# Graph attention with a layer norm in front: the normalisation moved from ScalarE to VectorE, and a batch of row statistics finished after the first weights

## The chip, the cores and the metric

The kernel runs on one core of one Trainium2 chip. The metric is the device time of one execution in microseconds (us). A core has TensorE (PE, matrix products and transposes), VectorE (DVE), ScalarE (ACT), GpSimd (POOL) and SyncE (SP); each works through its own list of instructions in order, and semaphores hold an instruction back until another engine has counted far enough. SyncE and GpSimd also start the transfers (DMA) between the chip's main memory and its on-chip memory (SBUF). PSUM is the memory that TensorE writes.

## The reference, cut to what matters

x is 8192 x 128, adj an 8192 x 8192 matrix of 0 and 1 (int32, about one entry in 512 is 1), W is 128 x 128 and a has 256 values.

```
h  = maximum(layernorm(x), 0)          # per row of 128, eps 1e-5
Wh = h @ W
f1, f2 = Wh @ a[:128], Wh @ a[128:]
e  = leaky_relu(f1[:, None] + f2[None, :], 0.2)
e  = where(adj == 0, -inf, e)
out = x + softmax(e, axis=1) @ Wh
```

## The kernel before, in words

**Tiling.** The 8192 rows are 64 tiles of 128, taken in 16 row groups of 4 tiles. The same 16 groups appear twice: as destination rows q (the rows of the output), and as source blocks b (the columns of adj that are summed over). For each pair (q, b), a "unit", TensorE transposes the adjacency marks of the block into PSUM (`transposes`, L266), VectorE turns them into weights with four instructions of 128 x 512 (`weights`, L601), and TensorE multiplies the weights with the features of the block and adds to four accumulators (`products`: 16 wide products of 258 columns at L277 and 16 of 129 columns at L281). There are 16 x 16 = 256 units.

**The first row of units, q = 0, also makes the features.** For a row group g the steps are, with the letters that the text uses:
- statistics (g): four `bn_stats` on VectorE, L548, on the loaded x.
- moments (k) and inverses (k): a batch k of groups is finished together. The batches are group 0; groups 1 to 3; 4 to 7; 8 to 11; 12 to 15. `moments` is five small VectorE instructions (L556 to L562), then ScalarE takes a logarithm and an exponential (`root`, L450 and L452), then `inverses` is four small VectorE instructions, each but the last waiting for the one in front (L570 to L575).
- normalise (g): four ScalarE activations of 128 x 128 float32 with a scale and a bias per partition, L395, from xm into one of two buffers xn. Buffer g mod 2 is free once group g-2 has been transposed.
- x_transposes (g): four PE transposes, L228. relu (g): one ScalarE instruction, L404.
- features (g, 0) and (g, 1): PE, L241, each followed by keep (g, h) on ScalarE, L410.
- exponentials (g): two ScalarE instructions, L422 and L423. pack (g): two small VectorE instructions, L583 and L584. spread (g): four PE transposes, L256. keep_row (g): ScalarE, L443.
- scaled (g): four ScalarE activations, L430. high_part (g): ScalarE, L437. low_part (g): VectorE, L592.

**What sets the order.** Each engine's order is written out by hand: a prologue, then `for b in range(UN)` with 16 turns, L319 for PE, L479 for ScalarE, L637 for VectorE. In turn b, here called block b, PE runs: transposes of block b+1, x_transposes (b+3), a wait for the weights and the pair of block b, then four parts of products with features (b+2, 0), spread (b+1) and features (b+2, 1) between them. spread (b+1) waits for pack (b+1) and for relu (b+3), because both write the same PSUM bank. ScalarE runs scaled (b+1), relu (b+3), high_part (b+1), keep (b+2, 0), keep_row (b+1), normalise (b+4), keep (b+2, 1), exponentials (b+2), and root at b = 3 and b = 7. VectorE runs statistics (b+8), weights (b+1), low_part (b+1), moments if b is 3 or 7, pack (b+2), inverses if b is 3 or 7. The batch of groups 4 to 7 has its statistics, moments and inverses in VectorE's prologue; ScalarE's root (2) for it stands in front of normalise (3) and of block 0's scaled (1) and relu (3).

**The loads.** SyncE loads x in five transfers, one for each batch; the fourth (groups 8 to 11) and the fifth are issued after the first four adjacency loads have landed (L158). GpSimd issues the adjacency loads, L181, 1 MB of int32 each, converted to 256 KB of bytes.

**The other rows of units,** q = 1 to 15, have no feature work: PE runs transposes of a block three ahead and the 32 products of a unit, VectorE the four weights, ScalarE copies the accumulators out (`evacuate`, L505).

Of the kernel before, what the change touches and what calls it, by code (L numbers as in the profile page):

```python
# [28 lines left out]
ALU = mybir.AluOpType  # L29
ACT = mybir.ActivationFunctionType  # L30
# [7 lines left out]
P = 128  # L38
PACK = 4
# [15 lines left out]
def gat_kernel(nc, x, adj, W, a, out):  # L55
# [3 lines left out]
    NQ = NB // PACK  # L59
# [10 lines left out]
    def batch_of(g):  # L70
        return next(k for k, (lo, hi) in enumerate(BATCHES) if lo <= g < hi)

    with ExitStack() as ctx:
# [10 lines left out]
        xm = sb("xm", [P, NQ, BANK], F32)  # L84
# [5 lines left out]
        xn = sb("xn", [P, 2, BANK], F32)  # L90
# [294 lines left out]
        @block.scalar  # L385
        def _(act):

            def normalise(g):

                act.wait_ge(s["ln_ready"], batch_of(g) + 1)  # L390
                if g >= 2:
                    act.wait_ge(s["xt_ready"], g - 1)
                for r in range(PACK):
                    t = g * PACK + r
                    mm = nc.scalar.activation(xn[:, g % 2, r * P:(r + 1) * P], xm[:, g, r * P:(r + 1) * P],  # L395
                                              ACT.Identity, scale=small[:, 5, t:t + 1], bias=small[:, 6, t:t + 1])
                mm.then_inc(s["xn_ready"], 1)

            def relu(g):

                act.wait_ge(s["xt_ready"], g + 1)
# [54 lines left out]
            act.wait_ge(s["wtp_ready"], 1)  # L456
            nc.scalar.activation(wt[:], acc[:, 0, 0:P], ACT.Copy).then_inc(s["wt_ready"], 1)
            root(0)
            normalise(0)
            nc.scalar.activation(squares, acc[:, 0, 0:P], ACT.Square,  # L460
                                 accum_out=lim[:, 2:3]).then_inc(s["norms_ready"], 1)
            relu(0)
            root(1)
            normalise(1)
            keep(0, 0)
            relu(1)
            keep(0, 1)
# [2 lines left out]
            high_part(0)  # L470
            keep_row(0)
            keep(1, 0)
            normalise(2)
            relu(2)
            keep(1, 1)
            exponentials(1)
            root(2)
            normalise(3)
            for b in range(UN):  # L479
                if b + 1 < NQ:  # L480
                    scaled(b + 1)
                if b + 3 < NQ:
                    relu(b + 3)
                if b + 1 < NQ:
                    high_part(b + 1)
                if b + 2 < NQ:
                    keep(b + 2, 0)
                if b + 1 < NQ:
                    keep_row(b + 1)
                if b + 4 < NQ:  # L490
                    normalise(b + 4)
                if b + 2 < NQ:
                    keep(b + 2, 1)
                    exponentials(b + 2)
                if b == 3 or b == 7:
                    root(3 + b // 7)
# [37 lines left out]
        def _(dve):  # L534
# [30 lines left out]
            def inverses(k):  # L565

                sl = slice(BATCHES[k][0] * PACK, BATCHES[k][1] * PACK)
                gap, both, total, root, square, rstd, shift = (small[:, n, sl] for n in range(7))
                dve.wait_ge(s["root_ready"], k + 1)
                then(nc.vector.tensor_tensor(square, root, root, ALU.mult))  # L570
                then(nc.vector.scalar_tensor_tensor(out=square, in0=square, scalar=-0.5, in1=both,
                                                    op0=ALU.mult, op1=ALU.mult))
                then(nc.vector.scalar_tensor_tensor(out=rstd, in0=square, scalar=1.5, in1=root,
                                                    op0=ALU.add, op1=ALU.mult))
                nc.vector.scalar_tensor_tensor(out=shift, in0=total, scalar=-0.5, in1=rstd,  # L575
                                               op0=ALU.mult, op1=ALU.mult).then_inc(s["ln_ready"], 1)


            def pack(g):

                dve.wait_ge(s["exps_ready"], g + 1)
                sl = slice(g * PACK, (g + 1) * PACK)
                then(nc.vector.tensor_scalar(packedv[:, sl, :, 1], exps[:, sl, :], CAP, CUT, ALU.min, ALU.mult))  # L583
                nc.vector.scalar_tensor_tensor(out=packedv[:, sl, :, 0], in0=exps[:, sl, :], scalar=CAP,  # L584
                                               in1=packedv[:, sl, :, 1], op0=ALU.min, op1=ALU.subtract
                                               ).then_inc(s["packed_ready"], 1)
# [30 lines left out]
            statistics(0)  # L617
            moments(0)
            inverses(0)
            dve.wait_ge(s["wap_ready"], 1)  # L620
            nc.vector.tensor_copy(wx[:, Fo:E1], acc[:, 1, 0:1]).then_inc(s["wx_ready"], 1)
            nc.vector.tensor_scalar(wx[:, E1:WC], acc[:, 1, 1:2], -1.0, None, ALU.mult).then_inc(s["wx_ready"], 1)
# [1 line left out]
                statistics(g)  # L624
            moments(1)
            inverses(1)
            pack(0)
            statistics(4)
            statistics(5)
            low_part(0)  # L630
            first_weights(0)
            pack(1)
            statistics(6)
            statistics(7)
            moments(2)
            inverses(2)
            for b in range(UN):  # L637
                if b + 8 < NQ:
                    statistics(b + 8)
                if b + 1 < NQ:  # L640
                    first_weights(b + 1)
                    low_part(b + 1)
                if b == 3 or b == 7:
                    moments(3 + b // 7)
                if b + 2 < NQ:
                    pack(b + 2)
                if b == 3 or b == 7:
                    inverses(3 + b // 7)
# [124 lines left out]
```

## Time and profile before

| what | value |
|---|---|
| time, median of 3 runs | 881.77 us (881.33 to 881.92) |
| the profiled execution's own time | 881.87 us |
| its span | 880.1 us |
| PE busy | 844.1 us, 96% of the span |
| VectorE busy | 756.4 us, 86% |
| ScalarE busy | 116.8 us, 13% |
| adjacency loads | 256 of 256 KB, 67.13 MB, 80.4% of 16 DMA engines' span |

The span is the time from the first to the last instruction of the profiled execution; its own time adds 1.77 us of what lies around. Busy shares are averages over the whole span. The stage in which the features are made fills the first 120.8 us, and in it ScalarE is busy most of the time; in the 742 us after it, ScalarE is nearly idle. "Idle before, released by" behind a row of a timeline means that the engine stood still for so long and what ended the wait. Rows that have "x4" are four instructions in a row: start of the first, then the length from there to the end of the last. An instruction's listed duration is about 0.08 us longer than the distance to the next one on VectorE, since they overlap at their ends.

### The profile page before, as it was taken

The page shows a single profiled execution, that of the slowest core. Times are in us where ns is not written, and L with a number is a line of the kernel's source. Part 1 is how long each engine was busy: PE and PEld are TensorE (multiplying, and loading weights), DVE is VectorE, ACT ScalarE, POOL GpSimd, SP SyncE. Part 2 cuts the span into 40 slices and gives each one's busy share as a digit, 9 for nine tenths or more (in the row PEclk, how much of TensorE's full clock was granted, in tenths as well). Part 3 has the DMA queues.
Part 4 walks back from the last instruction along what each step waited for, and adds up shares of the span by engine and source line. Part 5 has one row for each costly group of instructions (what it writes and reads, how often), then busy time and mean ns, then how long its engine had stood idle before and what let it go on. Part 6 is the DMA issues. An engine that isn't in the chain of part 4 may idle for free.

```text
span 880.1 us, 22961 instructions
## 1 busy us (share of the span) xinstructions
PE 844.1 (96%) x9475; PEld 773.2 (88%) x9475; DVE 756.4 (86%) x1287; ACT 116.8 (13%) x318; POOL 136.6 (16%) x263
## 2 busy tenths in 40 slices
PE   3699999999999999999999999999999999999995
PEld 2588899999999999999999999999999999999995
DVE  3588689898989889898989989898989989898985
ACT  4599930000000000000000000000000000000000
POOL 4000021111111111111111111111101110111000
PEclk9999999999999999999999999999999999999998
DMA  8995569899888988898899889988898989988400
GB/s 152 159 122 51 49 64 114 83 101 86 91 83 87 99 81 92 84 100 83 90 85 92 92 81 94 93 90 83 91 93 82 90 83 102 85 90 83 41 13 16
DMA packets 41740, 75.96 MB, mean 86 GB/s; under 512 B 4720, under 2 KB 4848, under 8 KB 41712
## 3 DMA queue, kind: packets, MB, share of 16 engines
q0 software_dynamic: 36864, 67.13, 80.4%
q1 hardware_dynamic: 4848, 8.46, 2.8%
q8 instruction: 18, 0.29, 0.1%
q14 instruction: 10, 0.08, 0.0%
HBM read 272.70 MB, written 4.19 MB: 315 GB/s over the span
## 4 chain that ended last, share of the span: by engine, by line
PE 88%; ACT 7%; issue 2%; DVE 2%; POOL 0%; DVEq 0%; POOLq 0%; ACTq 0%
PE acc L277 49%; PE acc L281 25%; PE stage L266 12%; ACT xn L395 3%; ACT tmp L430 1%; DVE wt_ring L601 1%; ACT wh L410 1%; ACT ht L404 1%; ACT pairs L437 1%; PE stage L241 1%; PE stage L228 1%; ACT exps L422 0%; PE stage L256 0%; ACT tmp L423 0%; DVE stats L548 0%
## 5 line engine op out<-in xcount | busy, mean ns | idle before, releaser
L601 DVE SCALAR_TENSOR_TENSOR wt_ring<-row,packed,stage 128x512 f32<-128x512 uint8 (+1 forms) x1024 | 695.4, 743 | 79.3 <-PE acc L281 68.2
L277 PE MATMUL acc<-pairs,wt_ring 128*128 128x258 f16 x4096 | 720.4, 274 | 0.4 <-DVE wt_ring L601 0.2
L281 PE MATMUL acc<-pairs,wt_ring 128*128 128x129 f16 x4096 | 698.5, 219 | 0.0
L277 PEld LDWEIGHTS acc<-pairs,wt_ring 128*128 128x128 f16 x4096 | 396.3, 97 | 55.6 <-DVE wt_ring L601 0.4
L281 PEld LDWEIGHTS acc<-pairs,wt_ring 128*128 128x128 f16 x4096 | 399.6, 98 | 4.9
L181 POOL DMA_DIRECT2D masks<-in_adj_dram x256 | 135.7, 536 | 658.2 <-PE stage L266 646.4
L266 PE MATMUL stage<-ident,masks 128*128 128x128 f32 x1024 | 155.0, 275 | 0.0
L505 ACT ACTIVATE fin<-acc 128x258 f32<-128x258 f32 x64 | 24.8, 387 | 730.2 <-PE acc L277 730.2
L266 PEld LDWEIGHTS stage<-ident,masks 128*128 128x128 f32 x1024 | 108.8, 141 | 3.7
L395 ACT ACTIVATE xn<-xm,small 128x128 f32<-128x128 f32 x64 | 26.2, 483 | 1.7 <-DVE small L575 1.7
L228 PE MATMUL stage<-ident,xn 128*128 128x128 f32 x64 | 12.3, 322 | 12.6 <-ACT xn L395 12.6
L241 PE MATMUL stage<-wx,ht 128*128 128x130 f32 x128 | 23.5, 311 | 0.7 <-ACT ht L404 0.7
L228 PEld LDWEIGHTS stage<-ident,xn 128*128 128x128 f32 x64 | 7.9, 159 | 15.6 <-ACT xn L395 15.6
L430 ACT ACTIVATE tmp<-wh,tmp 128x128 f32<-128x128 f32 x64 | 20.4, 390 | 0.4
L241 PEld LDWEIGHTS stage<-wx,ht 128*128 128x128 f32 x128 | 19.0, 213 | 1.6 <-ACT ht L404 1.1
L548 DVE BATCH_NORM_STATS2 stats<-xm 128x6 f32<-128x128 f32 x64 | 13.5, 279 | 7.3 <-DMA xm<-in_x_dram 7.3
L583 DVE TENSOR_SCALAR packed<-exps 128x8 f16<-128x8 f32 x16 | 2.8, 174 | 19.2 <-ACT tmp L423 19.2
L664 DVE SCALAR_TENSOR_TENSOR xm<-fin,inv,xm 128x128 f32 (+1 forms) x64 | 18.2, 348 | 0.0
L256 PE MATMUL stage<-ident,packed 128*128 128x128 f32 x64 | 10.8, 296 | 4.0 <-ACT ht L404 2.4
L654 DVE SCALAR_TENSOR_TENSOR fin<-fin 128x516 f32<-128x516 f32 x16 | 11.1, 691 | 3.4 <-ACT fin L505 3.4
L256 PEld LDWEIGHTS stage<-ident,packed 128*128 128x128 f32 x64 | 7.2, 147 | 6.8 <-issue 4.9
L410 ACT ACTIVATE wh<-stage 128x260 f32<-128x260 f32 x32 | 11.9, 371 | 2.9 <-PE stage L241 2.8
(44 smaller groups left out, 71.5 us busy)
## 6 DMA issues: line engine op xcount, KB each, us to landing
masks<-in_adj_dram POOLq DMA_DIRECT2D x256, 256.0 KB, 8.8
out_dram<-xm SPq DMA_DIRECT2D x16, 256.0 KB, 2.0
xm<-in_x_dram SPq DMA_DIRECT2D x3, 1024.0 KB, 17.5
xm<-in_x_dram SPq DMA_DIRECT2D x1, 768.0 KB, 6.4
xm<-in_x_dram SPq DMA_DIRECT2D x1, 256.0 KB, 2.6
wx<-in_L_gnn_W_dram SPq DMA_DIRECT2D x1, 64.0 KB, 2.4
a_sb<-in_L_gnn_a_dram SPq DMA_DIRECT2D x1, 1.0 KB, 3.8
```

Of the source, the lines that this page charges most:

```text
L181: nc.gpsimd.dma_start(masks[:, c * PACK + r, :], adj_dram[q, r, c]).then_inc(adj_loaded[c], 16)
L228: mm = nc.tensor.transpose(stage[:, 2, r * P:(r + 1) * P], xn[:, g % 2, r * P:(r + 1) * P], ident[:])
L241: mm = nc.tensor.matmul(stage[:, 3, r * 256:r * 256 + WC], ht[:, g % 2, k:k + P], wx[:], start=(r == 0), stop=(r == 1), skip_group_check=True)
L266: mm = nc.tensor.transpose(stage[:, bank, r * P:(r + 1) * P], words[:, c * PACK + r, kk * P:(kk + 1) * P], ident[:])
L277: return nc.tensor.matmul(acc[:, r, 0:2 * E1], wtv[:, w, r, 1, :], pairv[:, t, :, 0:E1], start=st, stop=end)
L281: return nc.tensor.matmul(acc[:, r, 0:E1], wtv[:, w, r, 0, :], pairv[:, t, 0, 0:E1], start=False, stop=False)
L395: mm = nc.scalar.activation(xn[:, g % 2, r * P:(r + 1) * P], xm[:, g, r * P:(r + 1) * P], ACT.Identity, scale=small[:, 5, t:t + 1], bias=s ...
L410: nc.scalar.activation(wh[:, t:t + 2, :], stage[:, 3, :].rearrange("p (r c) -> p r c", r=2)[:, :, 0:WC], ACT.Copy).then_inc(s["wh_ready"], 1)
L430: mm = nc.scalar.activation(tmp[:, g % 2, r, 0:Fo], wh[:, g * PACK + r, 0:Fo], ACT.Identity, scale=tmp[:, g % 2, r, Fo:E1])
L505: nc.scalar.activation(fin[:, r, :], acc[:, r, 0:2 * E1], ACT.Copy).then_inc(s["acc_free"], 1)
L601: nc.vector.scalar_tensor_tensor(out=wt_ring[:, t % NW, :], in0=e_row, scalar=packed[:, t, 1:2], in1=marks[:, k, :], op0=ALU.max, op1=ALU. ...
L664: nc.vector.scalar_tensor_tensor(out=o, in0=fin[:, r, 0:Fo], scalar=inv[:, r:r + 1], in1=o, op0=ALU.mult, op1=ALU.add).then_inc(s["rows_do ...
```

## The change

ScalarE's normalise is taken out at all its places and written as four VectorE `tensor_scalar` instructions, with the same waits and the same semaphore. In VectorE's prologue its order becomes: group 0 behind inverses (0), groups 1 and 2 behind inverses (1), group 3 behind the first weights; statistics (4) and (5) and low_part (0) are reordered around the first weights; inverses (2) leaves the prologue and goes behind weights (1) and low_part (1) in block 0. In the loop, statistics (b+8), which stood in front of the weights, goes behind them and behind normalise (b+4).

```diff
@@ ScalarE
-            def normalise(g):
-
-                act.wait_ge(s["ln_ready"], batch_of(g) + 1)
-                if g >= 2:
-                    act.wait_ge(s["xt_ready"], g - 1)
-                for r in range(PACK):
-                    t = g * PACK + r
-                    mm = nc.scalar.activation(xn[:, g % 2, r * P:(r + 1) * P], xm[:, g, r * P:(r + 1) * P],
-                                              ACT.Identity, scale=small[:, 5, t:t + 1], bias=small[:, 6, t:t + 1])
-                mm.then_inc(s["xn_ready"], 1)
-
...
-            normalise(0)
...
-            normalise(1)
...
-            normalise(2)
...
-            normalise(3)
             for b in range(UN):
...
-                if b + 4 < NQ:
-                    normalise(b + 4)
@@ VectorE
+            def normalise(g):
+
+                dve.wait_ge(s["ln_ready"], batch_of(g) + 1)
+                if g >= 2:
+                    dve.wait_ge(s["xt_ready"], g - 1)
+                for r in range(PACK):
+                    t = g * PACK + r
+                    ins = nc.vector.tensor_scalar(xn[:, g % 2, r * P:(r + 1) * P], xm[:, g, r * P:(r + 1) * P],
+                                                  small[:, 5, t:t + 1], small[:, 6, t:t + 1], ALU.mult, ALU.add)
+                ins.then_inc(s["xn_ready"], 1)
...
             inverses(0)
+            normalise(0)
...
             moments(1)
             inverses(1)
+            normalise(1)
+            normalise(2)
             pack(0)
+            low_part(0)
+            first_weights(0)
+            normalise(3)
             statistics(4)
             statistics(5)
-            low_part(0)
-            first_weights(0)
             pack(1)
             statistics(6)
             statistics(7)
             moments(2)
-            inverses(2)
             for b in range(UN):
-                if b + 8 < NQ:
-                    statistics(b + 8)
                 if b + 1 < NQ:
                     first_weights(b + 1)
                     low_part(b + 1)
+                if b == 0:
+                    inverses(2)
+                if b + 4 < NQ:
+                    normalise(b + 4)
+                if b + 8 < NQ:
+                    statistics(b + 8)
                 if b == 3 or b == 7:
                     moments(3 + b // 7)
```

## Rows read from the trace of the kernel before

**Rows 1.** Busy time by stretch: window, length, engines in the header's order, clock, DMA

```profile
core 0: us, PE busy (x) PEld busy (x) DVE busy (x) ACT busy (x) POOL busy (x), PEclk, DMA share, GB/s
0.00:42.40 42.40, 18.38 (x90) 15.42 (x91) 17.90 (x80) 20.27 (x55) 9.44 (x22) 1.00 0.95 154
42.40:108.60 66.20, 63.67 (x622) 56.12 (x620) 52.51 (x132) 64.75 (x182) 6.36 (x12) 1.00 0.72 78
...
120.80:863.00 742.20, 742.20 (x8547) 683.83 (x8546) 668.17 (x1040) 22.04 (x57) 118.72 (x225) 1.00 0.86 85
```

**Rows 2.** Timeline of PE, blocks 2, 10 and 13: start, length, what, idle before

```profile
47.81 0.60 PE L266 MATMUL stage<-ident,masks 128*128 128x128 f32 x4
50.63 0.22 PE L281 MATMUL acc<-pairs,wt_ring 128*128 128x129 f16 x1
51.03 0.62 PE L256 MATMUL stage<-ident,packed 128*128 128x128 f32 x4 [0.18 <-ACT ht L404]
...
92.42 0.60 PE L266 MATMUL stage<-ident,masks 128*128 128x128 f32 x4
...
109.00 0.60 PE L266 MATMUL stage<-ident,masks 128*128 128x128 f32 x4
```

**Rows 3.** Timeline of ScalarE: a normalise and the row behind it

```profile
46.66 1.64 ACT L395 ACTIVATE xn<-xm,small 128x128 f32<-128x128 f32 x4
48.21 0.36 ACT L410 ACTIVATE wh<-stage 128x260 f32<-128x260 f32 x1
```

**Rows 4.** Timeline of VectorE: a block, and the batch's moments and inverses

```profile
49.13 0.17 DVE L583 TENSOR_SCALAR packed<-exps 128x8 f16<-128x8 f32 x1 [1.13 <-ACT tmp L423]
...
49.42 0.87 DVE L548 BATCH_NORM_STATS2 stats<-xm 128x6 f32<-128x128 f32 x4
50.20 2.71 DVE L601 SCALAR_TENSOR_TENSOR wt_ring<-row,packed,stage 128x512 f32<-128x512 f32 x4
...
58.48 0.69 DVE L592 SCALAR_TENSOR_TENSOR pairs<-pairs,tmp 128x516 f16<-128x516 f16 x1
...
59.71 0.18 DVE L562 SCALAR_TENSOR_TENSOR small<-small 128x16 f32<-128x16 f32 x1
...
60.53 0.17 DVE L570 TENSOR_TENSOR small<-small 128x16 f32<-128x16 f32 x1
...
61.25 0.86 DVE L548 BATCH_NORM_STATS2 stats<-xm 128x6 f32<-128x128 f32 x4
```

**Rows 5.** Timeline of VectorE: four instructions of the new one's shape

```profile
133.76 1.14 DVE L664 SCALAR_TENSOR_TENSOR xm<-fin,inv,xm 128x128 f32 x4
```

**Rows 6.** Page, costliest groups: busy, mean ns of one, idle before

```profile
L395 ACT ACTIVATE xn<-xm,small 128x128 f32<-128x128 f32 x64 | 26.2, 483 | 1.7 <-DVE small L575 1.7
...
L548 DVE BATCH_NORM_STATS2 stats<-xm 128x6 f32<-128x128 f32 x64 | 13.5, 279 | 7.3 <-DMA xm<-in_x_dram 7.3
```

**Rows 7.** Timeline of PE at the start of the feature stage

```profile
24.61 1.11 PE L228 MATMUL stage<-ident,xn 128*128 128x128 f32 x4 [2.01 <-ACT xn L395]
...
26.39 1.91 PE L266 MATMUL stage<-ident,masks 128*128 128x128 f32 x8
35.08 1.12 PE L228 MATMUL stage<-ident,xn 128*128 128x128 f32 x4 [6.78 <-ACT xn L395]
```

**Rows 8.** SyncE's issue of the fourth x load, groups 8 to 11

```profile
L150 SPq DMA_DIRECT2D xm<-in_x_dram x1: 380/380/380, 21.6 to 21.6; - x1
```

**Rows 9.** Timeline of VectorE at the start of the feature stage

```profile
27.60 2.72 DVE L601 SCALAR_TENSOR_TENSOR wt_ring<-row,packed,stage 128x512 f32<-128x512 f32 x4 [4.74 <-PE stage L266]
...
30.53 1.64 DVE L548 BATCH_NORM_STATS2 stats<-xm 128x6 f32<-128x128 f32 x8
...
39.16 0.87 DVE L548 BATCH_NORM_STATS2 stats<-xm 128x6 f32<-128x128 f32 x4 [4.83 <-DMA xm<-in_x_dram]
```

**Rows 10.** Timeline of ScalarE: root of batch 2, and relu of group 3

```profile
33.03 0.21 ACT L450 ACTIVATE small<-small 128x16 f32<-128x16 f32 x1 [5.49 <-DVE small L562]
...
36.24 0.60 ACT L404 ACTIVATE ht<-stage 128x512 f32<-128x512 f32 x1
```

## The prediction

> **What bounds the kernel now.** I read the busy times by stretch first. They split the span at the feature stage: from 120.8 us on, PE is busy without a gap and ScalarE hardly works, and no line of the change runs there; from 42.4 to 108.6 us ScalarE is busy for 64.75 of 66.2 us, with PE at 63.67 and VectorE at 52.51 [rows 1]. So all the change can touch lies ahead of 120.8 us, and in its middle ScalarE sets the pace, with PE close behind.
>
> Next PE's timeline. Blocks 2, 10 and 13 begin (mask transposes, L266) at 47.81, 92.42 and 109.00, so a late block takes (109.00 - 92.42) / 3 = 5.53 us. Inside block 2 the last product before spread starts at 50.63, and spread starts at 51.03, behind ScalarE's relu [rows 2]. Products of this kind follow each other by 0.06 us, so PE stood for 51.03 - 50.69 = 0.34 us. PE's own work in a block is 5.53 - 0.34 = 5.19 us. This is the most that taking work from ScalarE can give here: 0.34 us a block, although a normalise holds ScalarE for 48.21 - 46.66 = 1.55 us [rows 3].
>
> Then VectorE's timeline. A block has pack 0.29 (49.13 to 49.42), statistics 0.78 (to 50.20), weights 2.63 (2.71 less the 0.08 by which listed times overlap), low_part 0.61, sum 4.31 us, and 1.13 us of waiting in front of pack. At the end of a batch it also has moments, 0.71 us (from 58.48 + 0.61 = 59.09 to 0.09 past the start of the last, 59.71) and inverses, 0.72 us (60.53 to 61.25); with a small wait, 1.47 together [rows 4].
>
> **The price of a normalise on VectorE** isn't in the trace. Nearest in shape are bn_stats, 128 x 128 float32 from one source, 0.78 / 4 = 0.195 us from start to start [rows 4], and L664, the same shape with a scalar per partition and two sources, (1.14 - 0.35) / 3 = 0.263 [rows 5]. I take 0.20, so 0.80 us for four, since one source is the nearer likeness. The upper end is 1.05 us. For the lower end, bn_stats less half of its 0.133 us of streaming (128 columns at the pace of the weights, whose 384 more columns than L664 cost 0.40) is 0.13, four 0.52. Farther up, ScalarE's own instruction has a mean of 483 ns, four 1.93 us [rows 6].
>
> The Trainium skill, "VectorE: DVE Perf Modes", section "The perf-mode tier table", says that a float32 tensor_scalar between SBUF operands runs at two elements a cycle; by that the sum would be the second case below, not the first. No row of before has such an instruction.
>
> **The start, step by step.** PE's x_transposes (2) waited 2.01 us for ScalarE's normalise and began at 24.61 [rows 7]. In the new order normalise (1) and (2) follow inverses (1) on VectorE, long before, so PE goes straight on at 22.6 and each step behind it moves up by 2.0: mask transposes from 26.39 to 24.4. The masks are there: SyncE issued its fourth x load, which waits for the first four adjacency loads, at 21.6 [rows 8]. Weights (0) move from 27.60 [rows 9] to 25.6 and end at 28.25. Normalise (0) and the earlier (1) gain nothing: what VectorE spends on group 0 (0.8) delays the statistics of groups 1 to 3 by as much as it then saves on group 1.
>
> Normalise (3) ends at 28.25 + 0.80 = 29.05, so x_transposes (3) starts at 29.1 instead of 35.08 [rows 7]. What is late next is spread (1), behind relu (3), which stands on ScalarE behind root (2), and that behind moments (2). VectorE, after 29.05: statistics (4), (5) 1.56, pack 0.29, statistics (6), (7) 1.56, moments 0.80 with its end, so 33.3, against 33.0 before. These statistics had stood partly in a free stretch and are now behind the weights: the move costs this. Before, relu (3) came 36.24 - 33.03 = 3.21 us behind root (2) [rows 10], of which 1.55 was normalise (3); now 33.3 + 1.66 = 35.0, and it ends at 35.5. PE, which did products from about 30, stands and takes up spread (1) at 35.65. From a spread to the next block it is 47.81 + 5.53 - 51.03 = 2.31 us at PE's full clock. The clock column reads 1.00 all through [rows 1], but four transposes of the same shape take 1.12 us at 35.08 [rows 7] and 0.60 at 47.81 [rows 2]: PE works here at its 1.2 GHz level, not at 2.4. So 4.6 us, and block 1 starts at 40.3 (at full clock 38.0).
>
> VectorE before waited 4.83 us for the fourth x load and did weights (1) only then [rows 9]. Now it does weights (1), low_part (1), inverses (2) and normalise (4) in that gap, about to 38.4. Statistics (8) begin at 39.16 as before, and weights (2) not before 39.16 + 0.78 + 0.29 = 40.24, nor before mask transposes (2), 40.3 + 0.7 + 0.14 = 41.15. I take 41.15.
>
> **The blocks.** VectorE needs 4.31 + 0.80 = 5.11 us a block, PE 5.19, ScalarE 5.53 - 1.55 = about 4.0. PE is the bound, with a hair of room on VectorE. The room to be late is small: weights (b+1) can start 0.68 into PE's block b, normalise (b+4) ends 4.12 later at 4.80, and x_transposes (b+4) want it at 5.19 + 0.54 = 5.73. That is 0.9 us. Two batches put 1.47 us into that queue, ahead of normalise (8) and (12).
> - Blocks from 1: 40.3, 45.7 (0.2 for the slow clock), 50.9, 56.1, 61.3. Weights (5) start 5.11 + 1.47 behind weights (4), 51.57, at 58.15; normalise (8) ends at 62.26, and x_transposes (8) wanted 61.8: PE waits 0.45.
> - Block 6 66.9, 7 72.1, 8 77.3. VectorE stays late by about 0.7: weights (9) at 80.06, normalise (12) ends 84.17, wanted at 83.02: PE waits 1.15. Block 10 starts at 82.48 + 5.19 + 1.15 = 88.8, before at 92.42 [rows 2]: 3.6 us gained.
> - Blocks 10 to 12 have no statistics and wait for nothing: 3 x 0.34 = 1.0 more. Behind block 13 the order is as it was.
>
> Sum: 4.6 us. All later work moves up as a whole. Against the profiled execution's 881.87 this gives 877.3; the median is 0.1 lower, so 877.2.
>
> **The rivals**, each against 881.87.
> 1. *The VectorE instruction is cheap, and PE alone sets the pace.* With 0.52 us a group VectorE needs 4.83 a block, catches up 0.36 after each batch, and x_transposes (8) and (12) find their data: block 10 at 45.7 + 8 x 5.19 = 87.2, gain 5.2 + 1.0 = 6.2, 875.7. If in addition PE's clock has risen by block 0, weights (2) start at 40.24, the first wait is VectorE's, and block 10 is at 85.5: gain 7.9, 874.0. For it: nothing in the trace excludes it. Against it: no row shows a one-source instruction faster than one column a cycle.
> 2. *VectorE becomes the bound.* At 1.05 us a group it needs 5.36 a block, and the chain from weights (2) to (9) is 7 of these and 2.94: normalise (12) ends at 86.0, block 10 starts at 90.7, gain 1.7 + 1.0 = 2.7, 879.2. For it: the row with the scalar per partition is this dear.
> 3. *The gain of the start is lost to the loads.* Statistics (8) now stand in front of nothing but pack (2) and weights (2), still a necessary step, tied to the fourth x load. It can be 0.9 us later at no cost, then every microsecond costs one. If it lands as much as 4.8 us later, 4.6 - 3.9 = 0.7 stays: 881.2, no change that can be told. A mechanism would be slower issue of the adjacency loads behind which it is queued. In "SBUF — State Buffer", section "SBUF: two separate sides", the Trainium skill states that a VectorE instruction in a two-port mode keeps GpSimd from writing load descriptors. No row of before shows it.
> 4. *Slower than before.* With x for four instructions, block 13 begins at 77.6 + 8x + 4.65 + 3 x 5.19 = 97.8 + 8x; it breaks even with 109.00 at x = 1.40, or 0.35 us each. The place is the wait of x_transposes (b+3) for normalise. At ScalarE's mean of 0.483, x is 1.93, block 13 at 113.2, 4.2 late: 886.1. Against it: no VectorE row of this size comes near.
>
> **How the numbers follow.** Forecast 0.50, rival 1 0.22, rival 2 0.13, rival 3 0.08, rival 4 0.07. A measurement of this kernel can tell about 0.2%, 1.8 us, from no change. Forecast, 1 and 2 are faster by more, 0.85; 3 is within, 0.08; 4 is slower, 0.07. The range runs from rival 1's lower value, 873.9, to a little past rival 2, 879.8, and leaves out 3 and 4.
>
> **What would show it.** Right: blocks 10 to 13 spaced 5.2 us, PE's waits at x_transposes now released by VectorE, longest at groups 8 and 12; x_transposes (3) near 29 and a wait before spread (1); weights (2) near 41; four normalise in 0.8 us. Wrong: rows of the new instruction outside 0.13 to 0.26 us apart, statistics (8) later than 40, or a part after 120.8 whose length isn't as before.

## The result, and the profile after

The changed kernel takes 880.11 us (median of 20 runs, 879.29 to 881.2). The kernel before, in 20 runs beside it, takes 881.46. The ratio is 0.9984 with a 95% interval of 0.9977 to 0.999: about 1.35 us faster, just inside the 0.2% that the prediction called no change. The forecast was 877.2 and the range ended at 879.8, so the gain is a third of the one forecast and the time lies outside the range. It came closest to the second rival, "VectorE becomes the bound", 879.2.

First the page of the changed kernel: its header, busy time by engine, and the new instruction among the costliest groups.

```profile
span 879.1 us, 22959 instructions
...
PE 842.6 (96%) x9475; PEld 773.6 (88%) x9475; DVE 772.7 (88%) x1351; ACT 94.1 (11%) x254; POOL 136.8 (16%) x263
...
L568 DVE TENSOR_SCALAR xn<-xm,small 128x128 f32<-128x128 f32 x64 | 17.7, 340 | 0.1
```

ScalarE lost 22.7 us of work and VectorE gained 16.3. One of the 64 new instructions takes 0.340 us; the forecast had put its price next to bn_stats' 0.279 [rows 6]. By stretch:

```profile
42.40:108.60 66.20, 61.62 (x625) 56.27 (x623) 62.40 (x174) 48.96 (x134) 6.36 (x12) 1.00 0.74 81
...
120.80:863.00 742.20, 742.20 (x8550) 683.77 (x8548) 668.05 (x1041) 21.60 (x56) 118.74 (x225) 1.00 0.86 85
```

In the middle of the feature stage ScalarE was the fullest engine with 64.75 of 66.2 us and VectorE had 52.51 [rows 1]; now VectorE has 62.40 and ScalarE 48.96. The long rest is as before. Next PE's timeline of the changed kernel: starts of blocks 1, 4, 5, 10 and 13 (L266), x_transposes (7) and (8) (L228), and spread (5) (L256).

```profile
41.40 0.61 PE L266 MATMUL stage<-ident,masks 128*128 128x128 f32 x4
...
56.59 0.61 PE L266 MATMUL stage<-ident,masks 128*128 128x128 f32 x4
57.42 0.66 PE L228 MATMUL stage<-ident,xn 128*128 128x128 f32 x4 [0.23 <-DVE xn L568]
...
61.26 0.62 PE L256 MATMUL stage<-ident,packed 128*128 128x128 f32 x4 [1.35 <-ACT ht L393]
...
63.56 0.60 PE L266 MATMUL stage<-ident,masks 128*128 128x128 f32 x4
64.66 0.65 PE L228 MATMUL stage<-ident,xn 128*128 128x128 f32 x4 [0.49 <-DVE xn L568]
...
92.86 0.60 PE L266 MATMUL stage<-ident,masks 128*128 128x128 f32 x4
...
107.86 0.61 PE L266 MATMUL stage<-ident,masks 128*128 128x128 f32 x4
```

Blocks 1 to 9 take (92.86 - 41.40) / 9 = 5.72 us each, a little more than before, where they took (92.42 - 42.46) / 9 = 5.55. There are waits released by VectorE in front of x_transposes, and one of 1.35 us that I had not foreseen, in front of spread, released by ScalarE's relu. It comes back at 84.85. Blocks 10 to 12, which have no statistics, take 5.00 each, where they had taken 5.53 [rows 2].

VectorE's timeline shows why: a whole block, then the turn in which a batch is finished.

```profile
47.56 2.72 DVE L595 SCALAR_TENSOR_TENSOR wt_ring<-row,packed,stage 128x512 f32<-128x512 f32 x4
50.20 0.69 DVE L586 SCALAR_TENSOR_TENSOR pairs<-pairs,tmp 128x516 f16<-128x516 f16 x1
50.80 1.11 DVE L568 TENSOR_SCALAR xn<-xm,small 128x128 f32<-128x128 f32 x4
51.83 0.86 DVE L531 BATCH_NORM_STATS2 stats<-xm 128x6 f32<-128x128 f32 x4
52.61 0.15 DVE L577 TENSOR_SCALAR packed<-exps 128x8 f16<-128x8 f32 x1
...
53.01 2.72 DVE L595 SCALAR_TENSOR_TENSOR wt_ring<-row,packed,stage 128x512 f32<-128x512 f32 x4
...
59.50 0.17 DVE L553 TENSOR_TENSOR small<-small 128x16 f32<-128x16 f32 x1 [0.24 <-ACT small L441]
...
60.25 2.72 DVE L595 SCALAR_TENSOR_TENSOR wt_ring<-row,packed,stage 128x512 f32<-128x512 f32 x4
```

From one block's weights to the next it is 53.01 - 47.56 = 5.45 us, with no wait inside; four normalise take 51.83 - 50.80 = 1.03. The turn with moments and inverses takes 60.25 - 53.01 = 7.24, that is 1.79 more.

### The profile page after: what moved, and what is told of

It is laid out like the page before. It is cut to its first block, busy times and chain, and to the rows that moved or that the text cites. A ratio compares the mean times of both kernels' runs of the same rounds, so it can differ in the third digit from the quotient of the medians.

```text
span 879.1 us, 22959 instructions
## 1 busy us (share of the span) xinstructions
PE 842.6 (96%) x9475; PEld 773.6 (88%) x9475; DVE 772.7 (88%) x1351; ACT 94.1 (11%) x254; POOL 136.8 (16%) x263
## 4 chain that ended last, share of the span: by engine, by line
PE 89%; DVE 7%; issue 2%; ACT 1%; POOL 0%; DVEq 0%; POOLq 0%; ACTq 0%
PE acc L277 50%; PE acc L281 25%; PE stage L266 12%; DVE wt_ring L595 3%; DVE xn L568 1%; DVE stats L531 1%; PE stage L241 1%; DVE pairs L586 1%; PE stage L228 0%; PE stage L256 0%; ACT tmp L419 0%; DVE packed L578 0%; DVE xm L665 0%; ACT small L439 0%; ACT small L441 0%
## 5 line engine op out<-in xcount | busy, mean ns | idle before, releaser
L266 PE MATMUL stage<-ident,masks 128*128 128x128 f32 x1024 | 154.9, 275 | 0.0
L266 PEld LDWEIGHTS stage<-ident,masks 128*128 128x128 f32 x1024 | 108.9, 141 | 3.7
L241 PE MATMUL stage<-wx,ht 128*128 128x130 f32 x128 | 24.0, 316 | 0.7 <-ACT ht L393 0.7
L228 PE MATMUL stage<-ident,xn 128*128 128x128 f32 x64 | 12.0, 319 | 9.6 <-DVE xn L568 9.4
L241 PEld LDWEIGHTS stage<-wx,ht 128*128 128x128 f32 x128 | 19.4, 217 | 1.6 <-ACT ht L393 1.1
L228 PEld LDWEIGHTS stage<-ident,xn 128*128 128x128 f32 x64 | 8.1, 160 | 12.2 <-DVE xn L568 11.8
L568 DVE TENSOR_SCALAR xn<-xm,small 128x128 f32<-128x128 f32 x64 | 17.7, 340 | 0.1
L256 PE MATMUL stage<-ident,packed 128*128 128x128 f32 x64 | 10.3, 285 | 6.5 <-ACT ht L393 5.0
L256 PEld LDWEIGHTS stage<-ident,packed 128*128 128x128 f32 x64 | 6.9, 141 | 7.6 <-issue 5.6
L586 DVE SCALAR_TENSOR_TENSOR pairs<-pairs,tmp 128x516 f16<-128x516 f16 x16 | 11.1, 692 | 1.7 <-ACT pairs L426 1.6
## 6 DMA issues: line engine op xcount, KB each, us to landing
xm<-in_x_dram SPq DMA_DIRECT2D x3, 1024.0 KB, 16.3
```

The lines of the kernel that those rows point to most:

```text
L228: mm = nc.tensor.transpose(stage[:, 2, r * P:(r + 1) * P], xn[:, g % 2, r * P:(r + 1) * P], ident[:])
L241: mm = nc.tensor.matmul(stage[:, 3, r * 256:r * 256 + WC], ht[:, g % 2, k:k + P], wx[:], start=(r == 0), stop=(r == 1), skip_group_check=True)
L266: mm = nc.tensor.transpose(stage[:, bank, r * P:(r + 1) * P], words[:, c * PACK + r, kk * P:(kk + 1) * P], ident[:])
L568: ins = nc.vector.tensor_scalar(xn[:, g % 2, r * P:(r + 1) * P], xm[:, g, r * P:(r + 1) * P], small[:, 5, t:t + 1], small[:, 6, t:t + 1], ...
L586: nc.vector.scalar_tensor_tensor(out=pairv[:, sl, 1, 0:E1], in0=pairv[:, sl, 0, 0:E1], scalar=-LOW, in1=tmp[:, g % 2], op0=ALU.mult, op1=A ...
```

## The experiments

Two theories stood against each other. **V**: VectorE's own work, 5.45 us a block and 1.79 per batch, paces blocks 1 to 9. **R**: the new wait of relu behind root on ScalarE, which waits for VectorE's moments, takes the gain. All ratios are to the kernel before, in runs beside it. They rest on twenty runs of the changed kernel and ten of each other one, but on seven for price_one and four for price_imm, price_wide, split22, split22_late and best22. "Block 1" and "block 13" are the starts of their mask transposes in the trace of one execution. Everything behind block 13 is alike: from there to the end it is 772.7 to 773.2 us in all fourteen. The changed kernel's profiled execution took 880.87 us, 0.76 above its median, so up to that much of any distance from its trace can be this one execution's.

| kernel | median us | ratio, 95% interval | block 1 | block 13 |
|---|---|---|---|---|
| before | 881.46 | 1 | 42.46 | 109.00 |
| changed | 880.11 | 0.9984 (0.9977 to 0.999) | 41.40 | 107.86 |
| order_only | 883.2 | 1.0011 (0.9998 to 1.0024) | 43.00 | 109.72 |
| norm_only | 883.8 | 1.0026 (1.0016 to 1.0036) | 37.03 | 111.18 |
| root_late_loop | 882.28 | 0.9999 (0.9989 to 1.0009) | 40.57 | 109.13 |
| root_late_all | 880.03 | 0.9981 (0.997 to 0.9991) | 37.07 | 108.08 |
| price_imm | 875.51 | 0.9926 (0.991 to 0.9943) | 40.31 | 103.40 |
| price_wide | 873.15 | 0.9902 (0.9886 to 0.9919) | 38.12 | 100.10 |
| split22 | 876.23 | 0.9947 (0.9926 to 0.9967) | 40.32 | 103.39 |
| split22_late | 875.66 | 0.9932 (0.9915 to 0.9949) | 36.03 | 102.38 |
| early_moments | 879.12 | 0.9973 (0.9964 to 0.9983) | 40.30 | 106.43 |
| price_one | 877.91 | 0.996 (0.9949 to 0.9972) | 39.74 | 105.11 |
| price_wide_ptr | 874.14, one run | | 38.75 | 101.14 |
| best22 | 873.96 | 0.9922 (0.9905 to 0.9938) | 35.24 | 100.94 |

**order_only.** The changed kernel's VectorE list without its normalise calls, and ScalarE as before:

```diff
@@ VectorE, against the changed kernel
-            normalise(0)
...
-            normalise(1)
-            normalise(2)
...
-            normalise(3)
...
-                if b + 4 < NQ:
-                    normalise(b + 4)
```

> Only VectorE's new order (statistics, moments and inverses moved); all normalising stays on ScalarE. Theory V (VectorE's own work, 5.45 us a block and 1.8 more per batch, is what paces blocks 1 to 9 of the changed kernel, so its gain comes from the order of the start, and the move of normalise gives nothing net): ScalarE paces the blocks as before at 5.53 us, moments (2) come 1.5 us later than before and hold normalise (3), so block 1 starts near 43.9 instead of 42.46 and the kernel is 0.5 to 2 us slower than before, about 882.8. Theory R (the new wait of relu (7) and (11) behind root on ScalarE takes the gain) says nothing else here.

Measured: ratio 1.0011, an interval that still holds 1, and block 1 at 43.00, where 43.9 was expected. So the new order alone gives nothing, and the sign of a small loss stays open. The cause foreseen is in the trace: root (2) on ScalarE starts 34.81 instead of 33.03 [rows 10] and x_transposes (3) follows only then.

```profile
34.81 0.21 ACT L450 ACTIVATE small<-small 128x16 f32<-128x16 f32 x1 [7.03 <-DVE small L562]
...
36.86 1.12 PE L228 MATMUL stage<-ident,xn 128*128 128x128 f32 x4 [8.33 <-ACT xn L395]
```

**norm_only.** The kernel before with ScalarE's calls taken out and VectorE's put in, while statistics, moments and inverses stay where they were:

```diff
@@ VectorE, against the kernel before
             inverses(0)
+            normalise(0)
...
             inverses(1)
+            normalise(1)
+            normalise(2)
...
             first_weights(0)
+            normalise(3)
...
                     low_part(b + 1)
+                if b + 4 < NQ:
+                    normalise(b + 4)
```

> VectorE normalises, but statistics, moments and inverses keep the order of before, so weights (1) again stand behind statistics (8), which wait for the fourth x load until 39.2 us. Theory V: VectorE starts weights (2) near 45.4 instead of 42.1 and is the bound from there, so 3 us slower than the changed kernel, about 883.2, 1.8 slower than before. Theory R: PE has room while it waits for relu, so less than 1.5 us of that delay reaches the end.

Measured: 883.8, 3.7 us slower than the changed kernel, with block 13 at 111.18 against 107.86. From VectorE and then PE:

```profile
38.40 0.87 DVE L531 BATCH_NORM_STATS2 stats<-xm 128x6 f32<-128x128 f32 x4 [4.91 <-DMA xm<-in_x_dram]
...
44.50 2.71 DVE L596 SCALAR_TENSOR_TENSOR wt_ring<-row,packed,stage 128x512 f32<-128x512 f32 x4
```

```profile
37.03 0.61 PE L266 MATMUL stage<-ident,masks 128*128 128x128 f32 x4
43.58 1.12 PE L228 MATMUL stage<-ident,xn 128*128 128x128 f32 x4 [5.94 <-DVE xn L569]
```

VectorE stands 4.91 us for the fourth x load before weights (1), weights (2) come at 44.50 instead of 42.11, and PE, which had begun block 1 early, at 37.03, stands 5.94 us for normalise (4). So weights (2) are 2.39 late and block 13 is 3.32 late, where R allowed less than 1.5 of the delay to reach the end. It is more than the delay itself: PE's granted clock was 0.50 of full speed from 43.6 to 48.5 us, behind its wait of 5.94, block 1 became long, and VectorE waited another 2.28 us in it for exponentials (3). That a delay of VectorE reaches the end is V's reading: neither half of the change pays alone, and together they do, because the new order fills the wait for the load that VectorE can't afford once it normalises.

**root_late_loop.** R's own test:

```diff
@@ ScalarE, against the changed kernel
                 if b + 1 < NQ:
                     high_part(b + 1)
+                if b == 4 or b == 8:
+                    root(3 + b // 8)
...
-                if b == 3 or b == 7:
-                    root(3 + b // 7)
@@ VectorE
                     low_part(b + 1)
-                if b == 0:
-                    inverses(2)
+                if b % 4 == 0 and b <= 8:
+                    inverses(2 + b // 4)
...
-                if b == 3 or b == 7:
-                    inverses(3 + b // 7)
```

> The changed kernel with root (3) and root (4) on ScalarE moved behind relu and high_part of blocks 4 and 8, and inverses (3) and (4) on VectorE behind the weights and low_part of those blocks. Spread (5) and (9) no longer wait for relu. Theory V: PE gets to x_transposes (8) and (12) earlier and waits there for VectorE; only VectorE's own two waits of 0.24 go, so the gain is 0.3 to 0.7 us, 879.5. Theory R: both waits of 1.5 us go, gain 3 us, 877.1.

Measured: no gain, neither R's 3 us nor V's 0.3 to 0.7. The ratio, 0.9999, is above the changed kernel's 0.9984, with intervals that touch. (One of its ten runs took 3105 us; it isn't in the ratio, and its cause wasn't looked into.) The wait before spread is gone and PE is at block 5's x_transposes earlier, where it now waits for VectorE:

```profile
61.20 0.60 PE L266 MATMUL stage<-ident,masks 128*128 128x128 f32 x4
63.72 0.66 PE L228 MATMUL stage<-ident,xn 128*128 128x128 f32 x4 [1.91 <-DVE xn L568]
65.43 1.18 PE L241 MATMUL stage<-wx,ht 128*128 128x130 f32 x4
67.69 0.61 PE L256 MATMUL stage<-ident,packed 128*128 128x128 f32 x4
```

R falls as the reason: x_transposes (8) follow weights (2) by 22.4 us here (63.72 - 41.28) and by 22.55 in the changed kernel (64.66 - 42.11), although nothing holds spread (5) any more. From weights (2) to weights (9) VectorE takes 41.33 us instead of 41.72: the 0.4 that V had counted on is there. What V hadn't foreseen is the row of L241, 1.18 us for what takes 0.66 in other blocks. Busy times and granted clock (third column from the right) by window:

```profile
55.00:61.00 6.00, 5.78 (x61) 5.20 (x60) 5.83 (x20) 4.63 (x14) 0.00 (x0) 1.00 1.06 107
61.00:63.50 2.50, 0.81 (x9) 0.55 (x6) 2.36 (x10) 1.89 (x7) 0.00 (x0) 1.00 1.07 107
63.50:66.00 2.50, 2.28 (x15) 2.03 (x16) 2.43 (x9) 1.13 (x2) 0.00 (x0) 0.66 1.06 107
66.00:68.00 2.00, 2.00 (x14) 1.68 (x14) 2.00 (x4) 0.39 (x1) 0.00 (x0) 0.58 0.36 44
```

Behind a wait of 1.91 us, PE's granted clock fell to its 1.2 GHz level and stayed there for some 3.5 us. From x_transposes to spread block 5 took 67.69 - 63.72 = 3.97 us instead of 66.99 - 64.66 = 2.33: the fall costs 1.6 us beside the wait itself. The same happens at x_transposes (12), so block 13 comes 1.27 us later than in the changed kernel.

**root_late_all.** In addition:

```diff
@@ ScalarE, against root_late_loop
-            root(2)
...
-                if b == 4 or b == 8:
-                    root(3 + b // 8)
+                if b % 4 == 0 and b <= 8:
+                    root(2 + b // 4)
```

> As root_late_loop, and root (2) too stands behind relu (3) and high_part (1). The wait of 2.3 us in front of spread (1) goes, and with it PE's fall to half clock behind it, so block 1 starts near 37 instead of 41.4. Theory V: weights (2) on VectorE can start only when statistics (8) and pack (2) are through, 41.1 to 41.8 against 42.11, so 0.3 to 1.0 us gain over root_late_loop, about 878.9. Theory R: the 4 us go straight into the time, about 873.

Measured: 880.03, the changed kernel's time again, so R's 873 is excluded. Block 1 starts at 37.07, 3.5 us ahead of root_late_loop, and block 13 only 1.05 ahead. That looks like V's 0.3 to 1.0 and isn't: weights (2) start at 41.22, as in root_late_loop (41.28), and weights (9) even 0.6 later. The distance comes from PE's clock. PE waits 1.91 us at x_transposes (8) and again at (12); behind the first its clock falls, behind the second it doesn't:

```profile
64.30:67.70 3.40, 3.38 (x19) 2.92 (x20) 3.33 (x10) 1.22 (x3) 0.00 (x0) 0.53 0.86 91
...
86.50:88.40 1.90, 0.06 (x1) 0.00 (x0) 1.76 (x10) 1.21 (x4) 0.00 (x0) 1.00 0.00 0
88.40:91.00 2.60, 2.54 (x26) 2.40 (x27) 2.53 (x7) 1.51 (x3) 0.00 (x0) 1.00 0.00 0
```

Block 5 takes 70.59 - 61.81 = 8.78 us and block 9, with the same wait, 93.08 - 85.95 = 7.13: one fall of the clock costs 1.65 us. In root_late_loop both blocks take 8.8. (The expectation of split22_late below says that PE fell to half clock behind each of the two waits; it fell behind one.) Taking waits off PE gives next to nothing while VectorE is full.

**price_imm** and **price_wide** make VectorE's normalise cheaper and leave the rest:

```diff
@@ VectorE, against the changed kernel: price_imm
-                                                  small[:, 5, t:t + 1], small[:, 6, t:t + 1], ALU.mult, ALU.add)
+                                                  1.0, 0.0, ALU.mult, ALU.add)
@@ price_wide, in place of the loop over r
+                ins = nc.vector.tensor_scalar(xn[:, g % 2, :], xm[:, g, :], 1.0, 0.0, ALU.mult, ALU.add)
```

> The changed kernel with constants 1.0 and 0.0 in place of the two scalars per partition of each VectorE normalise: same four instructions, but the rows are not normalised (h is made from x itself). Theory V (VectorE's 4.42 + 1.03 us a block pace blocks 1 to 9): what the scalars cost comes off eight blocks. If an instruction falls from 0.258 to 0.20 us apart, 7 x 0.24 = 1.7 us, 878.4; if it falls to 0.13, PE becomes the bound and it is 3 us, 877. Theory R (the wait of relu behind root): no change, 880.1. The Trainium skill, VectorE: DVE Perf Modes, section The perf-mode tier table, gives a float32 tensor_scalar between SBUF operands two elements a cycle, which would make the rows about 0.07 us shorter than bn_stats' 0.195 apart.

> As price_imm, but one VectorE instruction of 128 x 512 in place of four of 128 x 128. The rows are not normalised either. At one column a cycle it takes 0.60 us, at two 0.33. Theory V: VectorE needs 5.0 or 4.75 us a block, PE's 5.0 becomes the bound, the gain over the changed kernel is 2.5 to 4 us, 876 to 877.5. Theory R: no change.

Measured: 875.51 and 873.15, 4.6 and 7.0 us under the changed kernel, both more than V had said and far from R's none. The waits of spread for relu are still in price_imm's trace (0.79 and 1.25 us), so the gain comes without taking them away. From block 1 to block 13 the two kernels take 63.1 and 62.0 us, against 66.5 and PE's own 12 x 5.00 = 60: PE is nearly the bound, and now these waits are part of what is left above 60. In price_imm an instruction is 0.135 us apart, for which V had said 3 us; blocks 1 to 12 give 3.4, and another 1.1 is there at block 1 already (40.31 against 41.40), as are 3.3 of price_wide's 7.0. V had priced the blocks and not the start, where normalise (0) to (3) get cheaper too.

**price_one** and **price_wide_ptr** ask what that price consists of:

```diff
@@ VectorE, against the changed kernel: price_one
-                                                  small[:, 5, t:t + 1], small[:, 6, t:t + 1], ALU.mult, ALU.add)
+                                                  small[:, 5, t:t + 1], 0.0, ALU.mult, ALU.add)
@@ price_wide_ptr, in place of the loop over r
+                t = g * PACK
+                ins = nc.vector.tensor_scalar(xn[:, g % 2, :], xm[:, g, :],
+                                              small[:, 5, t:t + 1], small[:, 6, t:t + 1], ALU.mult, ALU.add)
```

> One scalar per partition (the scale) and the constant 0.0 for the other in VectorE's normalise; the shift by the mean is left out. price_imm's instruction takes 0.223 us, the changed kernel's 0.340. If each scalar per partition costs the same, 0.28 us, 0.20 apart, so VectorE needs 4.42 + 0.79 = 5.2 us a block and the kernel is near 877.5. If the first one alone takes the instruction out of the fast mode, 0.34 us and 880.

> One VectorE instruction of 128 x 512 with two scalars per partition (those of the group's first tile, so the other tiles are normalised with wrong numbers). price_wide without scalars took 0.432 us. If the scalars cost a fixed time, 0.12, it takes 0.55 us. If they halve the pace to one column a cycle, it takes 0.80 or more. Theory V: VectorE at about 4.9 us a block, near 874.

The grouped rows of the four kernels (busy time, then mean ns of one), in the order price_imm, price_one, price_wide, price_wide_ptr, one fence each:

```profile
L568 DVE TENSOR_SCALAR xn<-xm 128x128 f32<-128x128 f32 x64 | 10.0, 223 | 0.1
```

```profile
L568 DVE TENSOR_SCALAR xn<-xm,small 128x128 f32<-128x128 f32 x64 | 13.8, 282 | 0.1
```

```profile
L566 DVE TENSOR_SCALAR xn<-xm 128x512 f32<-128x512 f32 x16 | 6.8, 432 | 0.1
```

```profile
L567 DVE TENSOR_SCALAR xn<-xm,small 128x512 f32<-128x512 f32 x16 | 8.6, 545 | 0.1
```

Without scalars per partition 0.223 us, with one 0.282, with two 0.340: 0.06 each. At four times the columns the two cost 0.545 - 0.432 = 0.113, the same. And 384 more columns cost 0.432 - 0.223 = 0.21 us, where the weights' 384 columns more than L664's cost 0.40: two columns in the time of one. So the fast pace was there, and a fixed charge per scalar ate what it saves at 128 columns. By the Trainium skill's rule, "VectorE: DVE Perf Modes", section "The perf-mode tier table", float32 tensor_scalar between SBUF operands runs at two elements a cycle: the runs agree. In price_one four instructions take 0.78 us (44.15 to 44.93), VectorE's weights (5) to (8) follow each other by 5.21, and 877.91 fits V's 877.5.

```profile
44.15 0.87 DVE L568 TENSOR_SCALAR xn<-xm,small 128x128 f32<-128x128 f32 x4
44.93 0.87 DVE L531 BATCH_NORM_STATS2 stats<-xm 128x6 f32<-128x128 f32 x4
```

**split22** shares the work: VectorE takes two tiles of a group, ScalarE two. ScalarE's places are those of before with two exceptions, which the expectation doesn't name: normalise (2) stands right behind normalise (1), and normalise (3) in front of root (2).

```diff
@@ PE, against the changed kernel
                 pe.wait_ge(s["xn_ready"], g + 1)
+                pe.wait_ge(s["xa_ready"], g + 1)
@@ VectorE
-                for r in range(PACK):
+                for r in (0, 1):
@@ ScalarE, normalise again, with
+                for r in (2, 3):
...
+                mm.then_inc(s["xa_ready"], 1)
...
             root(1)
+            normalise(1)
+            normalise(2)
...
             exponentials(1)
+            normalise(3)
             root(2)
```

> Tiles 0 and 1 of each group are normalised by VectorE, 2 and 3 by ScalarE at the places of before, with a semaphore of its own; else the changed kernel. VectorE 4.42 + 0.52 = 4.94 us a block, ScalarE 4.0 + 0.8 = 4.8, PE 5.0. Theory V: PE paces the blocks; 66.5 us for blocks 1 to 12 become 62 to 63.5, block 1 starts 0.5 earlier: gain 3.5 to 5 us over the changed kernel, about 876. Theory R: the two waits of spread for relu stay and grow by what ScalarE has more to do, gain under 1.5 us.

Measured: 876.23. Blocks 1 to 12 take 103.39 - 40.32 = 63.1 us, as V said. The waits of spread for relu are 0.83 and 1.17 us, not longer than the changed kernel's 1.35, so ScalarE's added work cost nothing to see.

**split22_late** adds root_late_all's moves:

> split22 with root behind relu and high_part, and inverses behind low_part, as in root_late_all. In root_late_all PE's wait moved to x_transposes (8) and (12), 1.9 us each, and PE fell to its half clock behind each. Here VectorE has 0.5 us a block to spare and comes to inverses earlier, so the waits should be 1.0 to 1.4 and the clock stay up: 1 to 2 us less than split22, about 874.5. If the clock falls all the same, the same as split22 or slower.

Measured: 875.66, the intervals of the two overlap, so whether it is faster isn't settled. The forecast was 874.5. PE's waits at x_transposes (8) and (12) were 1.60 and 1.31 us, and the granted clock reads 1.00 behind both.

**early_moments** instead brings the moments forward:

```diff
@@ VectorE, against the changed kernel
-                if b + 8 < NQ:
-                    statistics(b + 8)
                 if b == 3 or b == 7:
                     moments(3 + b // 7)
+                if b == 0:
+                    statistics(8)
+                if b + 9 < NQ:
+                    statistics(b + 9)
```

> The changed kernel with statistics of groups 9 to 15 one block earlier and moments (3) and (4) in front of the statistics of their block, so that root does not hold relu on ScalarE. Nothing is taken off VectorE but its waits of 0.24 for root. Theory V: 0 to 0.7 us faster than the changed kernel, about 879.7, with PE's waits at spread (5) and (9) gone and longer ones at x_transposes (8) and (12), short enough (under 1.9) that PE's clock stays up. Theory R: 3 us faster, 877.

Measured: 879.12, 1.0 us under the changed kernel, with intervals that overlap: between V's 0.7 and a third of R's. The waits before spread (5) and (9) shrank from 1.35 to 0.44 and 0.45, and the clock stayed up (the column reads 1.00 from 42.4 to 108.6 us). From weights (2), at 41.76, to block 13 it takes 64.7 us instead of 65.75. This 1.1 is VectorE's own: statistics (9), 0.78 us, now stand ahead of weights (2), and one of its two waits of 0.24 for root is gone. So R's chain is tested here without a fall of the clock in between: 1.8 us of spread's waits are gone, and no gain beyond VectorE's is seen.

**best22** is split22 with early_moments' order and root (2) behind high_part (1):

```diff
@@ ScalarE, against split22
-            root(2)
...
                 if b + 1 < NQ:
                     high_part(b + 1)
+                if b == 0:
+                    root(2)
```

> split22 with the statistics and moments of early_moments, and root (2) behind relu (3) and high_part (1). VectorE 4.94, ScalarE 4.8, PE 5.0 us a block, and no wait of spread for relu in blocks 4 and 8 (0.8 and 1.2 us in split22); PE's wait of 2.9 in front of spread (1) goes, but VectorE's work in block 0 sets the start of weights (2) near 40. Theory V: PE paces all blocks, 60 to 61 us for blocks 1 to 12, the feature stage ends near 112 instead of split22's 115, 873 to 874.5, faster than any version so far that computes everything.

Measured: 873.96, ratio 0.9922 (0.9905 to 0.9938): the fastest that computes everything. Block 13 comes at 100.94, 8.1 us ahead of before. Not all came as foreseen: blocks 1 to 12 take 65.7 us, not 60 to 61, since PE starts block 1 at 35.24 and then waits for VectorE, and falls to half clock behind that wait of 2.26 us (spread takes 1.06 us):

```profile
35.24 0.61 PE L267 MATMUL stage<-ident,masks 128*128 128x128 f32 x4
38.10 0.63 PE L229 MATMUL stage<-ident,xn 128*128 128x128 f32 x4 [2.26 <-DVE xn L587]
...
41.38 1.06 PE L257 MATMUL stage<-ident,packed 128*128 128x128 f32 x4
...
44.34 0.60 PE L267 MATMUL stage<-ident,masks 128*128 128x128 f32 x4
```

From block 2 on it is (100.94 - 44.34) / 11 = 5.15 us a block, close to PE's 5.00.

## Why the prediction was wrong

The sign was right and the stage was right; VectorE's load was not. The sentence that failed is "PE is the bound, with a hair of room on VectorE": VectorE needs 5.45 us a block and PE 5.00.

**The price of a normalise on VectorE** is the step that failed first: "I take 0.20, so 0.80 us for four, since one source is the nearer likeness". It is 0.258 apart, 1.03 us for four. The likeness was wrong in both its parts: the instruction streams faster than bn_stats and pays for two scalars that bn_stats doesn't have. The upper end of 1.05, from L664, fits by luck: L664 has one scalar and streams at half the pace. price_one shows how much hangs on this term. Its four instructions take 0.78 us, nearly the forecast's 0.80, and its time is 877.91, 0.7 us from the 877.2 of the forecast: 2.2 of the 2.9 us by which the forecast missed are the price. The first rival (the prediction also calls it "the second case"), 0.13 apart and 875.7, had the pace right (0.135 with constants, price_imm); the scalars lift the price to twice that.

**VectorE's work around it** was mis-sized too. The rows of before gave 4.31 us a block; it is 5.45 - 1.03 = 4.42. Weights now follow directly on pack and start 0.21 us behind the start of its second instruction, where statistics, which stood between them before, started 0.08 behind it. A batch costs 1.79 instead of 1.47, of which 0.24 is VectorE's wait for root.

**PE's own work** was put at 5.19 us a block and is 5.00, because the rows of before hold a second wait for ScalarE that I overlooked. In every block from the second on x_transposes start 0.05 us behind the end of a normalise, 0.17 us a block (and 0.34 in front of spread):

```profile
91.28 1.64 ACT L395 ACTIVATE xn<-xm,small 128x128 f32<-128x128 f32 x4
92.97 0.66 PE L228 MATMUL stage<-ident,xn 128*128 128x128 f32 x4
...
L228 PE MATMUL stage<-ident,xn x12: 272/273/328, 93.0 to 104.4; 128*128 128x128 f32 x12
its engine sat idle before it (us, times) until:
  ACT xn L395: 0.5, 3
```

The last line says that PE stood idle for 0.5 us in three blocks until ScalarE's normalise was done. So "the most that taking work from ScalarE can give" was 0.51 us a block and not 0.34; and even at the forecast's own numbers, 5.11 us for VectorE against 5.00, VectorE was the bound.

**The sum, step by step.** Spread (1) starts at 37.45 instead of 35.65, 1.8 late. Of this, 0.94 is that PE's very first matmul is late in this execution (9.80 against 8.86; in the experiments it ranges from 8.75 to 9.67 with no relation to their edits), and 0.7 is the price, once each in normalise (0), (1) and (3). From spread (1) to block 1 it takes 3.95 us and not 4.6, since PE starts it at full clock, and weights (2) follow 0.71 and not 0.84 behind. So weights (2) start at 42.11 instead of 41.15: +1.0. From weights (2) to weights (9) it is 83.83 - 42.11 = 41.7 us instead of 38.9: +2.8, of which 7 x 0.23 = 1.6 is the price, 7 x 0.11 = 0.8 the gap and 0.6 the batches, less 0.2 that the forecast had added for PE's slow clock. Normalise (12) itself: +0.2. So block 10 starts at 92.86 instead of 88.8, later even than before's 92.42. Blocks 10 to 12 gave 1.6 and not 1.0, because both waits for ScalarE are gone from them. Feature stage in all: 1.14 us gained instead of 4.6.

**The start** went as told, its clock only in part: x_transposes (2) no longer wait for normalise; spread (1) waits for relu (3) behind root (2) and moments (2), 2.31 us in the trace. But I let PE stay at 1.2 GHz from before that wait, and in fact it had risen to full clock by 34.5 and fell again behind the wait.

**Missed:** in blocks 4 and 8 the same chain, moments, root, relu, spread, holds PE for 1.35 us. I had worked it out for block 0 and not carried it to the other batches. It cost almost no time, because VectorE, later still, was the bound behind it: early_moments takes two thirds of these waits away and gains no more than VectorE's list explains.

**The rivals.** The second was right, with weights (2) and the batches again too small. The first, PE as the bound, is what price_wide and split22 show when VectorE is relieved. The third and fourth didn't come: statistics (8) started at 40.34 without a wait for the load, GpSimd's issue of an adjacency load took 536 ns on the mean as before, and the break-even of 0.35 us apart was not reached.

## What to carry to other kernels

When work moves to an engine that is then nearly full, the price of the new instruction decides the sign of the result, times the number of its turns; look for a row with the same operand kinds (here scalars per partition), not only the same shape and number of sources. Where two engines have room for half a task and neither for the whole, split it by tiles: split22 gave three to four times the gain of the whole move. A wait chain found at one batch should be looked for at every batch, but here shortening it paid little while a fuller engine stood behind it. And an engine's own work in a block is its length less all of its waits, also those of a tenth or two that a timeline leaves out.

## What the runs showed of the hardware that was not expected

- A VectorE tensor_scalar of float32, 128 x 128 between SBUF tensors, takes 0.223 us with constants, and each scalar operand per partition adds 0.06 us, at 512 columns (0.113 for two) as at 128.
- PE's granted clock fell to its 1.2 GHz level behind waits of 1.91 us (both in root_late_loop, the first of two in root_late_all) and behind the waits of 2.26 to 2.52 us around block 1 in seven kernels, 2.31 in the changed one and 2.26 in best22 among them. It stayed at 2.4 GHz behind the second 1.91 of root_late_all and behind 1.60, 1.35 and 1.31, so the length of a wait alone doesn't tell: two waits of 1.91 us in one execution had different ends. A fall lasted 3 to 4 us of dense work and cost 1.65 us beside the wait (blocks 5 and 9 of root_late_all). In the changed kernel, windows around the wait before spread (1) show one:

```profile
33.00:35.20 2.20, 2.14 (x15) 1.68 (x13) 2.10 (x13) 0.01 (x1) 0.00 (x0) 0.68 1.06 172
35.20:37.50 2.30, 0.06 (x1) 0.09 (x2) 2.30 (x4) 2.27 (x8) 0.00 (x0) 1.00 1.06 175
37.50:39.50 2.00, 2.00 (x13) 1.67 (x14) 1.79 (x7) 1.19 (x3) 0.00 (x0) 0.58 1.06 156
39.50:41.00 1.50, 1.50 (x9) 1.31 (x9) 1.50 (x8) 0.50 (x2) 0.00 (x0) 0.50 1.05 178
```
